# A layer of graph attention with a residual and two norms: half of the scores' cross products by a transpose, batches staged further ahead

## The reference

```
u     = h @ h.T / sqrt(384)                      # 256 x 256 scores, symmetric
p     = softmax(u);  delta = p * adjacency
attn  = delta / (sum of delta over the row + 1e-10)
ctx   = upper(attn) @ (h @ W_left.T + b_left)    # j > i
      + diag(attn) * (h @ W_self.T + b_self)
      + lower(attn) @ (h @ W_right.T + b_right)  # j < i
g     = relu(norm(ctx) * gamma + beta)
out   = norm(x + g)                              # norm: over the 384 features
```

## Time and profile before

| | us |
|---|---|
| median of 3 runs | 502.08 (501.5 to 502.15) |
| the profiled execution | 501.96 |
| its span | 500.0 |
| TensorE busy | 480.4 (96%) |
| VectorE busy | 342.6 (69%) |
| ScalarE busy | 333.3 (67%) |
| GpSimd busy | 217.5 (43%) |

### The profile page before, as it was taken

One profiled execution on the slowest core, in us unless ns is written; L12 is line 12 of the kernel. 1 busy time (PEld: TensorE's weight loads), 2 busy tenths in 40 slices (PEclk: granted clock), 3 DMA queues, 4 the chain that ended last, 5 costly groups with the idle time before them and its releaser, 6 DMA issues.

```text
span 500.0 us, 9525 instructions
## 1 busy us (share of the span) xinstructions
PE 480.4 (96%) x2902; PEld 477.4 (95%) x2902; DVE 342.6 (69%) x886; ACT 333.3 (67%) x738; POOL 217.5 (43%) x295
## 2 busy tenths in 40 slices
PE   7599999999999999999999999999999999999983
PEld 6599999999999999999999999999999999999972
DVE  2457766677776667777666777666777766677666
ACT  4367667666766766776777676676768667667742
POOL 0215554334555334455433445543345553344552
PEclk9599999999999999999999999999999999999998
DMA  8561344533344443344444234444434444433111
GB/s 244 187 209 50 102 141 151 160 116 113 128 140 136 157 156 95 116 137 146 136 157 152 92 113 141 144 145 157 129 103 124 137 136 157 157 123 108 41 69 63
DMA packets 63905, 65.90 MB, mean 132 GB/s; under 512 B 4752, under 2 KB 59792, under 8 KB 63888
## 3 DMA queue, kind: packets, MB, share of 16 engines
q1 hardware_dynamic: 63888, 65.69, 40.8%
HBM read 44.70 MB, written 20.97 MB: 131 GB/s over the span
## 4 chain that ended last, share of the span: by engine, by line
PE 93%; DMA 2%; DVE 1%; POOL 1%; ACT 1%; issue 1%; SPq 1%; POOLq 0%; DVEq 0%
PE ps_proj L322 58%; PE ps_ctx L358 20%; PE ps_scores L322 14%; DMA w_raw<-in_L_gnn_W_right 2%; POOL scaled L755 0%; DVE w_lo L599 0%; SPq L277 0%; ACT w_hi L458 0%; POOL dt_left L745 0%; ACT ps_scores L397 0%; POOL shifted L759 0%; DVE xt_lo L512 0%; POOL dt_right L745 0%; DVE delta L522 0%; ACT normed L433 0%
## 5 line engine op out<-in xcount | busy, mean ns | idle before, releaser
L322 PE MATMUL ps_proj<-w_hi,xt_hi 128*128 128x384 f32 x576 | 194.8, 338 | 6.2 <-DVE w_lo L599 3.8
L322 PE MATMUL ps_proj<-w_lo,xt_hi 128*128 128x384 f32 x576 | 194.4, 337 | 0.0
L322 PE MATMUL ps_proj<-w_hi,xt_lo 128*128 128x384 f32 x576 | 194.3, 337 | 0.0
L751 POOL TENSOR_TENSOR rstd<-var_eps,minus_half 128x4 f32<-128x4 f32 x32 | 32.5, 1015 | 211.9 <-DVE var_eps L571 209.4
L415 ACT ACTIVATE proj_hi<-ps_proj 128x384 fp32r<-128x384 f32 x128 | 62.7, 491 | 92.3 <-PE ps_proj L322 92.3
L322 PEld LDWEIGHTS ps_proj<-w_hi,xt_hi 128*128 128x128 f32 x576 | 108.9, 189 | 7.2 <-DVE w_lo L599 4.3
L411 ACT ACTIVATE ps_proj<-bias 128x384 f32<-128x384 f32 (+1 forms) x192 | 94.3, 493 | 29.9 <-DVE proj_lo L541 26.8
L322 PEld LDWEIGHTS ps_proj<-w_lo,xt_hi 128*128 128x128 f32 x576 | 108.9, 189 | 0.0
L322 PEld LDWEIGHTS ps_proj<-w_hi,xt_lo 128*128 128x128 f32 x576 | 108.8, 189 | 0.0
L541 DVE TENSOR_TENSOR proj_lo<-ps_proj,proj_hi 128x384 fp32r<-128x384 f32 x128 | 67.3, 544 | 59.4 <-ACT proj_hi L415 59.3
L755 POOL TENSOR_TENSOR scaled<-normed,gamma_sb 128x384 f32<-128x384 f32 x62 | 63.0, 1016 | 35.5 <-ACT normed L433 35.5
(11 more groups left out here) (73 smaller groups left out, 723.7 us busy)
## 6 DMA issues: line engine op xcount, KB each, us to landing
xt_sb<-in_x_t SPq DMA_DIRECT2D x32, 384.0 KB, 3.6
x_sb<-in_x SPq DMA_DIRECT2D x32, 384.0 KB, 4.2
out_dram<-out_sb SPq DMA_DIRECT2D x31, 384.0 KB, 2.7
adj_sb<-in_adj SPq DMA_DIRECT2D x32, 256.0 KB, 4.3
dt_dram<-turned SPq DMA_DIRECT2D x32, 256.0 KB, 2.0
dt_raw<-dt_dram SPq DMA_DIRECT2D x128, 64.0 KB, 2.0
w_raw<-in_L_gnn_W_left SPq DMA_DIRECT2D x1, 576.0 KB, 4.3
w_raw<-in_L_gnn_W_right SPq DMA_DIRECT2D x1, 576.0 KB, 9.6
```

Of the source, the lines that this page charges most:

```text
L322: mm = nc.tensor.matmul(to, stationary, moving, start=(k == 0 and not seeded), stop=(k == len(passes) - 1), skip_group_check=seeded)
L751: nc.gpsimd.tensor_tensor(rstd[at.slot(2)][:], var_eps[:], minus_half[:], ALU.pow).then_inc(rstd_ready, 1)
```

## The change

- Scores of batches from 1 on: TensorE computes only high x low (`cross`, 6 matmuls, two batches ahead, behind projection 4), VectorE transposes it in 32 x 32 blocks out of PSUM (`turn_cross`), SyncE stores it to a second DRAM tensor and loads it back in four loads (`cross_raw`). TensorE adds high x high on top of the same bank (`squares`, 6 matmuls, at the start of a batch for the next). `finish_scores` on VectorE adds the transposed cross product, scales by -SCALE and takes the minimum of each row in one instruction per tile; it takes the place of `maxima` and of the small `neg_max` copy on ScalarE. Batch 0 keeps all 18 matmuls and adds zeros. The moving operand of all scores matmuls is read in another order of columns (`keys`), and `deltas` puts the order back, in two instructions.
- There are two banks of scores; `ps_warm` is gone.
- VectorE and ScalarE split the deltas ahead of projection 0; VectorE puts the residuals of projections 2 and 3 behind `turn` and ahead of `residual`, and `diagonal` late. `x_t` is split three batches ahead.
- ScalarE: `exps` between projections 1 and 2 and ahead of seeds 4 and 5; `seed_ctx` 0 ahead of the next batch's seed 0. In batch 0 `exps(1)` stands ahead of `seed_ctx` 0.
- GpSimd: `triangles` ahead of both betas and of gamma of tile 1.
- SyncE: outputs are stored three batches behind, first in `one`; then the loads; then stores of deltas and of cross, then the eight loads back.

```diff
@@ SyncE
+            def store_turned(at):
                 sp.wait_ge(turned_ready, at.n(1, 1))
                 sp.dma_start(dt_dram[:], turned[:]).then_inc(turned_stored, 16)
+            def load_turned(at):
                 sp.wait_ge(turned_stored, at.n(16, 16))
                 for q in range(Q):
                     sp.dma_start(dt_raw[...], dt_rows[q]).then_inc(dt_loaded, 16)
+            def store_cross(at):
+                sp.wait_ge(cross_turned_ready, at.n(1, 0))
+                sp.dma_start(cross_dram[:], cross_turned[:]).then_inc(cross_stored, 16)
+            def load_cross(at):
+                sp.wait_ge(cross_stored, at.n(16, 0))
+                for q in range(Q):
+                    sp.dma_start(cross_raw[...], cross_rows[q]).then_inc(cross_loaded, 16)
...
             def one(at):
+                nxt, ahead, third = at.plus(1), at.plus(2), at.plus(3)
+                if at.plus(-3).exists(BATCHES):
+                    store(at.plus(-3))
+                if third.exists(BATCHES):
+                    if at.plus(-1).exists(BATCHES):
+                        sp.wait_ge(xt_lo_ready, at.n(1, 0))
+                    load_xt(third.n(1), third.slot(UNROLL))
+                if ahead.exists(BATCHES):
+                    if at.plus(-2).exists(BATCHES):
+                        sp.wait_ge(y_ready, at.n(T, -T))
+                    load(ahead.n(1), ahead.slot(UNROLL))
                 if nxt.exists(BATCHES):
+                    store_turned(nxt)
+                if ahead.exists(BATCHES):
+                    store_cross(ahead)
+                if nxt.exists(BATCHES):
+                    load_turned(nxt)
+                if ahead.exists(BATCHES):
+                    load_cross(ahead)
@@ TensorE
+            def keys(tile):
+                return tile.rearrange("p (h q c) -> p q h c", q=Q, c=R)
+            def cross(at):
+                pe.wait_ge(xt_lo_ready, at.n(1, 1))
+                if at.b != 1:
+                    pe.wait_ge(delta_ready, at.n(T, -T))
+                for t in range(T):
+                    for c in range(C):
+                        mm = nc.tensor.matmul(ps_scores[at.slot(2)][:, t, :], xt(at, c, t * P, (t + 1) * P)[0], keys(xt(at, c, 0, L)[1]),
+                                              start=(t == 0 and c == 0), stop=(c == C - 1), skip_group_check=True)
+                mm.then_inc(cross_ready, 1)
+            def squares(at):
+                pe.wait_ge(cross_turned_ready, at.n(1, 0))
+                for t in range(T):
+                    for c in range(C):
+                        mm = nc.tensor.matmul(ps_scores[at.slot(2)][:, t, :], xt(at, c, t * P, (t + 1) * P)[0], keys(xt(at, c, 0, L)[0]),
+                                              start=False, stop=(c == C - 1), skip_group_check=True)
                 mm.then_inc(scores_ready, 1)
...
             def one(at):
+                nxt, ahead = at.plus(1), at.plus(2)
+                if at.b != 0 and nxt.exists(BATCHES):
+                    squares(nxt)
                 for i, g in enumerate(order(at)):
                     project(at, g)
-                    if i == 1 and nxt.exists(BATCHES):
-                        scores(nxt)
                     if i == 3 and last(at):
                         attend(at, 0)
+                    if at.b == 0 and g == 3:
+                        cross(nxt)
+                    if at.b == 0 and g == 4:
+                        squares(nxt)
+                    if g == 4 and ahead.exists(BATCHES):
+                        cross(ahead)
@@ ScalarE
             def exps(at):
-                act.wait_ge(row_max_ready, at.n(1, 1))
-                nc.scalar.activation(neg_max[:], row_max[:], ACT.Copy, scale=-SCALE).then_inc(neg_max_ready, 1)
-                act.wait_ge(neg_max_ready, at.n(1, 1))
+                act.wait_ge(neg_max_ready, at.n(T, T))
...
             def split_delta(at):
                 act.wait_ge(dt_loaded, at.n(64, 64))
+                if at.b != 0:
+                    act.wait_ge(ctx_ready, at.n(T, 0))
...
+                if at.b == 0:
+                    split_proj(at, 0)
+                    split_delta(at)
+                else:
+                    split_delta(at)
+                    split_proj(at, 0)
                 if before.exists(BATCHES):
                     normalise(before)
                 split_proj(at, 1)
+                if at.b != 0 and nxt.exists(BATCHES):
+                    exps(nxt)
                 seed_proj(at, 4)
+                split_proj(at, 2)
                 seed_proj(at, 5)
-                if nxt.exists(BATCHES):
-                    exps(nxt)
-                split_proj(at, 2)
...
                 split_proj(at, 3)
-                if nxt.exists(BATCHES):
-                    seed_proj(nxt, 0)
+                if at.b == 0:
+                    exps(nxt)
                 if not last(at):
                     seed_ctx(at, 0)
                 if nxt.exists(BATCHES):
+                    seed_proj(nxt, 0)
@@ VectorE
+            def turn_cross(at):
+                dve.wait_ge(cross_ready, at.n(1, 0))
+                if at.b != 1:
+                    dve.wait_ge(cross_stored, at.n(16, -16))
+                nc.vector.transpose(cross_turned[:].rearrange("p (k t r) -> p t k r", t=T, r=R),
+                                    ps_scores[at.slot(2)][:].rearrange("p t (k c) -> p t k c", c=R)
+                                    ).then_inc(cross_turned_ready, 1)
+            def finish_scores(at):
+                if at.b != 0:
+                    dve.wait_ge(cross_loaded, at.n(64, 0))
                 dve.wait_ge(scores_ready, at.n(1, 1))
-                nc.vector.reduce_max(row_max[:], ps_scores[:], AX).then_inc(row_max_ready, 1)
+                nc.vector.memset(gate[:], 0.0)
+                for t in range(T):
+                    ps = ps_scores[at.slot(2)][:, t, :].rearrange("p (q e) -> p q e", q=Q)
+                    other = cross_raw[:, :, t, :]
...
+                    nc.vector.tensor_tensor_reduce(ps, ps, other, -SCALE, LARGEST, ALU.add, ALU.min, neg_max[:, t:t + 1]
+                                                   ).then_inc(neg_max_ready, 1)
...
             def one(at):
                 if before.exists(BATCHES):
                     context_stats(before, 1)
                     norm_variances(before)
                     norm_var_eps(...)
+                    split_delta(at)
+                    norm_shift(before)
                 split_proj(at, 0)
+                if at.b == 0:
+                    split_delta(at)
+                    for g in range(1, NSPLIT):
+                        split_proj(at, g)
+                    turn_cross(nxt)
                 if nxt.exists(BATCHES):
+                    finish_scores(nxt)
+                if at.b != 0:
+                    split_proj(at, 1)
+                if nxt.exists(BATCHES):
+                    deltas(nxt)
+                    turn(nxt)
+                if at.b != 0:
+                    split_proj(at, 2)
+                    if not last(at):
+                        split_proj(at, 3)
                 if before.exists(BATCHES):
                     residual(before, 0)
                     residual_stats(before, 0)
+                if ahead.exists(BATCHES):
+                    turn_cross(ahead)
                 if before.exists(BATCHES):
                     residual(before, 1)
                     residual_stats(before, 1)
+                if nxt.exists(BATCHES):
+                    diagonal(nxt)
+                if third.exists(BATCHES):
+                    split_xt(third)
...
@@ GpSimd
                     power(before)
-                    gamma_of(before, 0)
-                    beta_of(before, 0)
                 pool.wait_ge(dt_lo_ready, at.n(1, 1))
                 if before.exists(BATCHES):
-                    gamma_of(before, 1)
+                    gamma_of(before, 0)
                 triangles(at)
                 if before.exists(BATCHES):
+                    beta_of(before, 0)
+                    gamma_of(before, 1)
                     beta_of(before, 1)
```

More of the change, by code:

```diff
@@ L278, in _ @@
                     sp.dma_start(adj_sb[0][:], adj_rows[0]).then_inc(adj_loaded[0], 16)
-                    sp.dma_start(xt_sb[1][:], xt_rows[1]).then_inc(xt_loaded[1], 16)
+                    load_xt(1, 1)
             for to, vector in ((gamma_sb, gamma), (beta_sb, beta)):
                 sp.dma_start(to[:], vector.partition_broadcast(P)).then_inc(vectors_loaded, 16)
[L282 to L287, removed]
+            load_xt(2, 2)
+            sp.dma_start(x_sb[0][:], x_rows[0]).then_inc(x_loaded[0], 16)
+            load(1, 1)
+            first = Batch(0, 0)
+            store_turned(first)
+            load_turned(first)
+            store_cross(first.plus(1))
+            load_cross(first.plus(1))
             def store(at):
@@ L460, in _ @@
             split_xt(first.plus(1))
+            split_xt(first.plus(2))
             def one(at):
```

(23 more changed lines are left out.)

71 lines of the change are left out of this document (35 added, 36 removed).

## The result

The changed kernel takes 485.52 us (median of 4 runs, 485.02 to 486.24) against 502.12 beside it: the ratio is 0.9658 with the interval [0.9615, 0.9701]. The forecast of 486.5 was 1.0 us high. The profiled execution took 486.24 us, its span 484.5.

A forecast was written before the change was run, and what follows sets the result against it. TensorE alone was taken to bound the steady stretch, so fewer matmuls meant less time: 501.96 - 22.1 + 7.3 (start) - 0.8 (end) = 486.4, stated as 486.5 us (483 to 490; 8 in 10: 480.5 to 496.5).

The forecast's parts named there:

- TensorE saves 22.1 us: Scores of 31 batches: six fewer matmuls each at 0.119 us; a batch falls from 14.68 to 13.97 us.
- rivals 4 and 5: 4: permuted operand costs TensorE time, 500 to 530, chance 0.03; 5: weight loads pace its matmuls, same time, chance 0.02.
- New work on VectorE: Per batch: add-and-minimum 0.41 us each, 0.9 for both; transpose out of PSUM 0.71; VectorE's sum 11.7 of 13.97.
- (a): Steady batch: projection 4's seed on ScalarE, behind `exps`, ends at 5.9 us; TensorE wants it at 6.8, slack 0.9.
- The meeting on the port: VectorE's split of the deltas may meet GpSimd's power; the seed some 0.3 us later, slack of (a) 0.6.
- Rival 1: Projection 4's bank comes late in every batch: 492.5 us, or 498 if VectorE's end adds 0.2; chance 0.14.
- (c): Cross product's way through DRAM: 5.6 us from end of transpose to landing, slack 1.3 us before `finish_scores`.
- rival 2: The DRAM trip becomes the bound, a closed loop of 12.6 us that may reach 15.0, giving 517; chance 0.09.
- (e): Steady batch: context seeds are ready at 9.1 and 11.4 us, wanted by TensorE at 10.6 and 12.2.
- The start, +7.3: Batch 0: TensorE waits about 3, 1 and 5 us, low clock adds 1.5; ends at 42.9 instead of 35.61.
- rival 3: The start costs nothing, since batch 0's waits overlap otherwise than laid out: 479 us; chance 0.10.
- The end, -0.8: Last batch: triangles now ahead of the betas, so the first context goes 1.0 us earlier; gain 0.8.

The follow-up runs named there:

- e1: The changed kernel with the six low x high matmuls put back in `squares`, so 18 scores matmuls again: 506.64 us.
- e11: The changed kernel with six memsets of 256 elements into unused tiles on VectorE ahead of `finish_scores`: 507.38 us.
- e7: The changed kernel with `norm_shift` ahead of the split of the deltas on VectorE: 485.22 us.
- e5: The changed kernel with four more loads of 64 KB, read by nothing, ahead of the four cross loads: 499.73 us.
- e6: The changed kernel with eight more loads, read by nothing, ahead of the cross loads: 557.93 us.
- e2: The kernel before, with low x high left out of the scores of batches 1 to 31 (12 matmuls), nothing moved: 483.42 us.
- e9: The kernel before with 12 scores matmuls from batch 1 on, and `seed_ctx` 0 ahead of the next batch's seed 0 on ScalarE: 480.43 us.
- e4: The changed kernel with all 18 scores matmuls in batch 1 too, and `exps(1)` behind `seed_ctx` 0 in batch 0: 478.96 us.
- e10: e4 with the deltas of batch 0 split last, and `seed_ctx` 0 again behind `exps(1)`: 476.09 us.
- e12: The changed kernel run once more, unchanged: 487.12 us, beside 502.38 for the kernel before.
- e3: The changed kernel with `seed_ctx` 0 ahead of `exps(1)` in batch 0: 486.95 us.
- e8: The changed kernel with 26 matmuls that add zeros behind projection 5 of batch 0: 486.74 us.

## Why the prediction was right, step by step

- **TensorE saves 22.1 us.** Right: the middle stretch is 21.99 shorter, and e1 gives 21.1 back. The permuted operand costs nothing, 0.119 us a matmul; rivals 4 and 5 are out.
- **New work on VectorE.** An add-and-minimum takes 0.43 to 0.47 against 0.41, its read 0.14 against 0.08, both together 0.87 against 0.9, the transpose 0.72 against 0.71.
- **(a) Slack of the bank of projection 4.** 0.9 foretold; the seed ends at 258.57 and TensorE takes the bank at 259.39, 0.8 later, and e11 says 0.93. The meeting on the port came and costs the power 0.4, but VectorE's next large step needs `proj_hi` of projection 0, which ends at 255.40 whatever the power does; `shift` comes at 255.45. So the 0.3 feared for the seed was not paid, `finish_scores` starts 3.4 us into the batch, as foretold, and e7 changes nothing. Rival 1 counted the new instructions at twice their price, which they don't have. It is the thinnest cover, as e11 shows: from 0.93 us on, each tenth costs 3 us in all.
- **(c) The trip through DRAM.** 5.8 us against 5.6, the loop 12.3 against 12.6. The median landing of the 124 cross loads is 2.0, as it was for `dt_raw` before, and the longest is 3.2; the loads land 1.6 us ahead of `finish_scores`, so rival 2 didn't come. The Trainium skill (DMA: Bandwidth & Descriptors, Latency and other measured facts) gives 2 us for an HBM access at high load; as an addition to the landing, which is how the prediction took it, it was not seen at a mean DMA share of 0.55. e5 and e6 show that the trip is a bound some 1.7 us further on.
- **(e) Seeds.** Taken as given, and right. In the order of before it would not have been: with 12 matmuls the batch was 14.09 there (e2), 13.97 with the swap of the seed and the next batch's first bank (e9), which is 3 us in all. Whether the changed kernel too needs the swap no run shows.
- **The start, +7.3.** Measured +7.33, but by errors that cancel, which is luck. The waits were foretold as about 3, 1 and 5 us and were 2.04, 0.69 and 4.62. `turn_cross(1)` ended at 29.06 instead of 29.6 and `finish_scores` and what follows came 0.3 sooner still, so the contexts began at 36.98 and not 37.8: 0.8 less. The second seed, for which 0.4 was added, held nothing up. The clock was to cost 1.5 and cost 2.8 (5.96 less 3.17): 1.3 more. The range of 0 to 3 held it, but no row gave the 1.5. The row that it leans on was also misread: in the kernel before it is not 4 us of idleness that stand ahead of the 18 scores matmuls but 1.49; a gap of 3.78 lies further back, at 16.47, ahead of nine projection matmuls.
```profile
21.21 0.58 PE L322 MATMUL ps_scores<-xt_hi 128*128 128x256 f32 x1 [1.49 <-DVE xt_lo L512]
```
  That the trip is the reason for the start's price is shown by e4 (6.6 us less without it); rival 3 is out.
- **The end, -0.8.** Measured -0.84, from a first context 1.03 earlier in its batch.

## What to carry to other kernels

A trip that is hidden in the steady batch is not hidden in the first one, where nothing runs beside it: here the start gave back 7.3 us of 22.1. Computing batch 1 too in the old, direct way, and splitting the deltas of batch 0 late (e4, e10), got 9.4 of 485.5 us back (11.0 against the changed kernel in the same group, e12) at a price of six matmuls. When the engine that bounds gets faster, an order that cost nothing before can begin to cost time: put what that engine wants first ahead of what it wants last (e9), and measure what slack is left by adding a known dose of work (e11). Cutting one link of a chain of waits is worth nothing as long as the next tile hangs on the same one (e3).

## What the runs showed of the hardware that was not expected

- After 4.62 us of idleness the granted clock was 0.50 for the next 5.6 us, and 18 context matmuls took 5.96 us instead of 3.17; matmuls with zeros in the gap kept it at 1.00 (e8).
- With eight more loads (e6) single steady batches had a granted clock of 0.90 or 0.91 and took 17.6 to 18.6 us, beside 15.7 to 15.95 at 1.00.
- Meetings of VectorE and GpSimd turn on 0.3 us: the same `y_sb` takes 0.59 or 1.37 us by whether it starts 0.26 ahead of GpSimd's addition or 0.06 behind.
- Six memsets of 128x256 took 1.64 us, 0.27 each, more than the dose I had meant to give.
